# A graph network on one NeuronCore: a limit of two indirect DMAs in flight from GpSimd

## What is computed

```
L0:  radial = exp(coeff * (distance - offsets)^2)                  # 50 per edge
     h   = silu([x[src], x[dst], radial] @ Wm1 + bm1)
     h   = silu(h @ Wm2 + bm2);  message = h @ Wm3 + bm3
     out = segment_sum(message, dst)
     x   = layernorm(x + mlp([x, out]))                            # Wu1, Wu2, Wi1, Wi2
L1:  xt  = logmap0(x)
     att = sigmoid([xt[src], xt[dst], edge_attr_128] @ att_w + att_b)
     sup = xt + segment_sum(xt[src] * att, src)
              + mean by src of edge_attr_128 + mean by dst of edge_attr_128
     x   = layernorm(x + proj(expmap0(sup)))
```

## Time and profile before, and how to read it

| | |
|---|---|
| median of 3 runs | 2708.51 us (2707.11 to 2714.91) |
| profiled execution, span from first to last instruction | 2669.9 us |
| time outside the span, by difference to the median | 38.6 us |
| mean granted TensorE clock | 0.761 |
| busy: PE, DVE, POOL, ACT | 66%, 63%, 56%, 51% |
| DMA queue of POOL (software): packets, bytes, share of 16 engines | 50176, 104.07 MB, 13.2% |
| DMA queue of SP: packets, bytes, share | 283474, 233.47 MB, 33.7% |

### The profile page before, as it was taken

How to read it: one execution, slowest core, us unless ns; L and a number is a source line. 1 busy time by engine, 2 the same in 40 slices (tenths; PEclk the granted TensorE clock), 3 DMA queues, 4 the chain that set the end, 5 groups by cost and what they waited for, 6 DMA issues and landing times.

```text
span 2669.9 us, 41647 instructions
## 1 busy us (share of the span) xinstructions
PE 1766.1 (66%) x11127; PEld 1530.4 (57%) x11127; DVE 1679.0 (63%) x5490; ACT 1361.0 (51%) x3965; POOL 1498.9 (56%) x1572
## 2 busy tenths in 40 slices
PE   5677777777878787776643244777775666576770
PEld 5466665655666666565533233677665656576660
DVE  5666666666666677776535334788765555466668
ACT  3666665665666666875425333666643233233224
POOL 3566666665666666655566665566555455555510
PEclk8788888898888778997755556677777677777795
DMA  7465655654333233333433335566555455455541
GB/s 192 122 148 124 150 131 130 148 133 111 88 84 86 84 86 85 87 83 103 133 89 100 87 105 140 160 187 186 171 155 151 147 154 152 142 168 167 172 136 49
DMA packets 337140, 341.98 MB, mean 128 GB/s; under 512 B 67402, under 2 KB 266948, under 8 KB 336898
## 3 DMA queue, kind: packets, MB, share of 16 engines
q1 hardware_dynamic: 283474, 233.47, 33.7%
q0 software_dynamic: 50176, 104.07, 13.2%
q10 hardware_dynamic: 3248, 1.71, 0.3%
HBM read 246.14 MB, written 90.15 MB: 126 GB/s over the span
## 4 chain that ended last, share of the span: by engine, by line
PE 30%; DVE 20%; issue 17%; another core or an unknown queue 15%; ACT 11%; DVEq 3%; SPq 0%; DMA 0%; ACTq 0%
PE bank L1651 8%; PE bank L1010 5%; PE bank L1630 4%; PE bank L1311 3%; DVEq L758 3%; PE bank L1284 3%; PE bank L1324 3%; DVE rt L987 2%; ACT L1093 2%; ACT L779 2%; ACT ring L1093 1%; PE bank L1320 1%; DVE ring L1184 1%; DVE ring L978 1%
## 5 line engine op out<-in xcount | busy, mean ns | idle before, releaser
L933 POOL DMA_INDIRECT gtab<-ring,idx x784 | 753.9, 962 | 556.3 <-ACT ring L952 238.9
L1060 POOL DMA_INDIRECT ra<-ptab,gis x784 | 744.9, 950 | 491.6 <-issue 199.7
L1010 PE MATMUL bank<-ring 128*128 128x78 f32 x1568 | 299.9, 341 | 284.0 <-issue 220.9
L949 ACT ACTIVATE rt<-rt 128x254 f32<-128x254 f32 x536 | 215.4, 403 | 470.7 <-DVE rt L989 347.6
L1010 PEld LDWEIGHTS bank<-ring 128*128 128x128 f32 x1568 | 278.0, 258 | 306.6 <-issue 251.0
L1284 PEld LDWEIGHTS bank<-ring 128*128 128x128 f32 x1568 | 232.9, 215 | 175.9 <-issue 153.8
L1073 ACT ACTIVATE ring<-bank 128x512 f32<-128x512 f32 x196 | 116.3, 594 | 395.3 <-remote 349.0
L1284 PE MATMUL bank<-ring 128*128 128x78 f32 x1568 | 238.1, 293 | 103.4 <-issue 86.4
L1651 PE MATMUL bank<-ring 128*128 128x130 f32 x1312 | 230.7, 332 | 86.5 <-issue 67.2
L1630 PE MATMUL bank<-rt 128*128 128x126 f32 x1072 | 196.6, 328 | 108.0 <-issue 73.8
L1311 PEld LDWEIGHTS bank<-wm,ring 128*128 128x128 f32 x1568 | 250.7, 228 | 25.5 <-issue 10.9
(11 more groups left out here) (274 smaller groups left out, 3817.3 us busy)
## 6 DMA issues: line engine op xcount, KB each, us to landing
ring<-in_edge_attr SPq DMA_DIRECT2D x196, 256.0 KB
ring<-gtab SPq DMA_DIRECT2D x89, 393.0 KB
gtab<-ring SPq DMA_DIRECT2D x36, 687.8 KB
ra<-in_edge_weight SPq DMA_DIRECT2D x132, 128.0 KB
ring<-gtab SPq DMA_DIRECT2D x49, 327.5 KB
ring<-reld SPq DMA_DIRECT2D x196, 78.0 KB
ring<-gtab SPq DMA_DIRECT2D x49, 262.0 KB
ra<-ptab,gis POOLq DMA_INDIRECT x784
```

The costliest lines, as they stand in the source:

```text
L933: G.indirect_dma_start(out=gtab[group_of(i)][:, :], out_offset=bass.IndirectOffsetOnAxis(ap=idx[:, n, i:i + 1], axis=0), in_=row[i % NE][: ...
L949: k = S.activation(prl[i % NPR][:, n, :], prl[i % NPR][:, n, :], ACT.Identity, accum_out=lgs[i % 2][:, n:n + 1])
L1010: k = T.matmul(bk[:, 256:256 + W], row[i % NE][:, n, 0:H], od2[i % NO2][:, n, :], start=(first and n == 0), stop=(n == 3), skip_group_chec ...
L1060: G.indirect_dma_start(out=gp[i % NGP][:, n, :], out_offset=None, in_=ptab[:, :], in_offset=bass.IndirectOffsetOnAxis(ap=gis[:, n, i:i + 1 ...
```

## The change

FLY = 2 is new. Each indirect DMA of POOL now has a semaphore by its sub-tile n (0 to 3) in the place of one by its buffer, and ahead of each, POOL waits for the landing of the DMA two before it of the same kind. PE waits for each sub-tile just ahead of its transpose; SP's waits for scatters go by the four new semaphores.

```
+FLY = 2
...
-LAYER = (... tuple(f"gp{i}" for i in range(NGP))
+LAYER = (... tuple(f"gp{i}" for i in range(4))
...
-ROWS = (... tuple(f"sc{i}" for i in range(NE)) ...
+ROWS = (... tuple(f"sc{i}" for i in range(4)) ...
...
         def row_load(e, i):
             e0 = edge0(i)
             if i >= NE:
-                e.wait_ge(s[f"sc{i % NE}"], 64 * (i // NE))
+                slots_done(e, i - NE)
                 e.wait_ge(s["rp"], i - NE + 1)
...
         def slots_done(e, i):
-            for j in range(NE):
-                if i >= j:
-                    e.wait_ge(s[f"sc{j}"], 64 * ((i - j) // NE + 1))
+            for n in range(4):
+                e.wait_ge(s[f"sc{n}"], 16 * (i + 1))
...
+        def landed(e, name, k):
+            if k >= 0:
+                e.wait_ge(s[f"{name}{k % 4}"], 16 * (k // 4 + 1))
...
         def rows_pool(e, i):
...
             for n in range(4):
+                landed(e, "sc", 4 * i + n - FLY)
                 G.indirect_dma_start(
                     out=gtab[group_of(i)][:, :], out_offset=bass.IndirectOffsetOnAxis(ap=idx[:, n, i:i + 1], axis=0),
-                    in_=row[i % NE][:, n, :], in_offset=None).then_inc(s[f"sc{i % NE}"], 16)
+                    in_=row[i % NE][:, n, :], in_offset=None).then_inc(s[f"sc{n}"], 16)
...
         def layer_pool(e):
...
                     for n in range(4):
+                        landed(e, "gp", 4 * i + n - FLY)
                         G.indirect_dma_start(
                             out=gp[i % NGP][:, n, :], out_offset=None, in_=ptab[:, :],
-                            in_offset=bass.IndirectOffsetOnAxis(ap=gis[:, n, i:i + 1], axis=0)).then_inc(s[f"gp{i % NGP}"], 16)
+                            in_offset=bass.IndirectOffsetOnAxis(ap=gis[:, n, i:i + 1], axis=0)).then_inc(s[f"gp{n}"], 16)
...
         def layer_pe(e):
...
-                    e.wait_ge(s[f"gp{i % NGP}"], 64 * (i // NGP + 1))
                     for n in range(4):
+                        e.wait_ge(s[f"gp{n}"], 16 * (i + 1))
                         T.matmul(bk[:, n * P:(n + 1) * P], v[:, n, :], ident, start=(n == 0), stop=False, is_transpose=True,
                                  skip_group_check=True)
```

More of the change, by code:

```diff
@@ L174 @@
        "acc0", "lim") + tuple(f"pt{i}" for i in range(6))
-LAYER = (tuple(f"rb{i}" for i in range(3)) + tuple(f"qw{i}" for i in range(NQW)) + tuple(f"gp{i}" for i in range(NGP))
+LAYER = (tuple(f"rb{i}" for i in range(3)) + tuple(f"qw{i}" for i in range(NQW)) + tuple(f"gp{i}" for i in range(4))
          + tuple(f"wb{i}" for i in range(4))
@@ L180 @@
          "abt", "abc", "abw")
-ROWS = (tuple(f"ea{i}" for i in range(NE)) + tuple(f"sc{i}" for i in range(NE)) + tuple(f"wn{i}" for i in range(NWN))
+ROWS = (tuple(f"ea{i}" for i in range(NE)) + tuple(f"sc{i}" for i in range(4)) + tuple(f"wn{i}" for i in range(NWN))
         + ("odr", "bwp", "dm", "lb", "rp", "acce", "zacc"))
```

## The result

| | before | after |
|---|---|---|
| median | 2707.81 us (2692.44 to 2714.91, 4 runs) | 3064.18 us (3060.88 to 3067.35, 4 runs) |
| ratio | | 1.132, 95% interval 1.129 to 1.136 |
| span of the profiled execution | 2669.9 us | 3061.3 us (its own time 3063.1) |
| first gather, last gather, last scatter | 32.5, 1236.0, 2546.1 us | 32.0, 1481.9, 2955.1 us |

The kernel became 13% slower. The forecast was 2627 us, with a range up to 2880. By the starts in POOL's time line the gathers take 246 us more, the scatters (with the seam ahead of them) 163 us more, the end behind them 18 us less and the start 0.5 us less: together the 391 us between the spans. The medians are 356 us apart, since the profiled execution of before was quicker than any of the timed ones.

What follows compares the result with a forecast made beforehand. Taken as bound: indirect DMA issue at about 1.5 us, all sequencers late after some six in a row. +8 - 10 - 15 - 64 = -81 us gave a span of 2589, plus 38.6 outside it 2627 us; range 2370 to 2880.

Steps and rivals of the forecast that it cites:

- The bound before: All engines: after some six indirect DMAs in a row, sequencers see waits and instructions late until the DMAs have drained.
- Step (2): POOL's new wait: landing seen 2.24 us behind the start, so free at 2.50 us until the crawl begins.
- rival C: POOL's new wait always sees landings late, released when all in flight landed: pace 1.75 us, 2938 us; chance 0.27.
- part (5): SP's row loads L896 and unit loads L1414 wait on four semaphores: costs nothing, covered by SP's own idle time.
- Step (3): Shorter crawl where POOL paces, 1.51 us per DMA: gathers 0, scatters -10, -15 and -64 us.
- wrong altogether: Sign against the forecast: the crawl stays as long with two in flight, or DVE's pauses outlast POOL's.
- Step (1): POOL's wait ahead of 1566 of 1568 indirect DMAs: 0.01 us each when satisfied, 16 us in all, 8 per stage.
- Step (4): PE waits four times instead of once ahead of the transposes L1320, 588 more waits: at most 6 us, beside POOL's pace.
- Step (6): The prologue of 33 us and the 123 us behind the last scatter stay.
- 38.6 us "outside the span": Whole run: median 2708.51 lies 38.6 us above the profiled span, taken as time outside it and added to 2589.
- B: POOL in both stages: the crawl was the whole reason for 1.5 us, so pace 1.26 us, 2370 us; chance 0.20.
- D: Nothing moves: the wait is never late, or gathers give back what scatters win; 2709 us; chance 0.11.

Runs made afterwards that it cites:

- base: The kernel before, without any edit, run once more for a trace on a chip of 2120 us: 2122.0 us, ratio 1.0005.
- fly1: The changed kernel with FLY = 1, each indirect DMA waiting for the landing of the one just before: 5055.8 us, 2.384 times the kernel before.
- halfrows1: The changed kernel with FLY = 1 and each gather fetching only the first 64 of its 128 rows: 4991.5 us in a single execution.
- after2: The changed kernel, without any edit, on a chip where the kernel before takes 2121.1 us: 3063.9 us, ratio 1.442.
- fly4: The changed kernel with FLY = 4, so four in flight with the same waits and semaphores: 2280.9 us, 1.075 times the kernel before.
- chunk2: The kernel before with its own semaphores and one wait per chunk, chunk i for chunk i - 2, five to eight in flight: 2676.3 us, ratio 0.999.

## Why the prediction was wrong, step by step

**The bound before** was read half right. On the first chip POOL issues behind its own rate and all engines crawl behind some six DMAs in a row; base shows the same program without any of it. I took this for a law of the program, and so for something that the change could cure.

**Step (2) is the step that failed.** I took "as seen by a sequencer after four", 0.94 + 1.30 = 2.24 us, for the landing time, and so the wait for free at 2.50 us. That pause was the end of a wait for `h1p`, which PE raises; no landing was in it. fly1 shows the true size: a gather that flies alone lands a median of 2.56 us behind its start and the next starts 0.26 us later, 2.8 us in all, or 3.3 us over a chunk's seam. Even an undisturbed landing is late at 2.50 us. The trace before held no wait of POOL for a landing, so it bounded the price from below only (1.73 us, when the bytes move), and I placed it too near that end. Measured: in the changed kernel POOL is held in 62% of the gathers (225 of 362 and 242 of 392, counting gaps over 0.45 us), and there the release comes a median of 3.37 us (beside the fills) and 3.31 us (behind them) behind the start of the DMA waited for; in the scatters 3.74 us up to 1860 us and 3.85 us behind, never under 2.68. The break-even that rival C named, a landing seen over 3.2 us behind its start, was right, and the measured values lie beyond it.

The page of the Trainium skill that the prediction set beside this ("DMA: Bandwidth & Descriptors", section "Anatomy of one DMA — SWDGE (gpsimd) path") gives 2.0 us fixed plus the bytes, 2.15 us for 64 KB; fly1's gathers measure 2.56 us from start to landing. With halfrows1's 2.41 us that makes 0.15 us for 32 KB and some 2.26 us fixed. In kind the page is off here: it says that most of the fixed part is waiting for the write to be confirmed, but in fly1 the first byte of a gather moves a median of 1.65 us behind the start (1.54 for a scatter) and the landing comes 0.34 to 0.40 us behind the last byte. Most of the time lies ahead of the transfer.

**What I had not in the sum at all: the fills.** The row of L1041 was on the page (36 of 687.8 KB), and in the ticks of the gathers; part (5) looked at SP's queue and found it covered. The cover was POOL's lead of six chunks. With two in flight 39 waits of over 3 us in the gathers are paid in full: the gathers are 2.04 us apart beside the fills, 1.68 behind them. Of the 246 us that the gathers lost, (2.04 - 1.51) x 400, about 210, were lost in the stretch with the fills. The fills' own part is the distance to the quiet pace: (2.04 - 1.68) x 400, about 140 us by this estimate. The rest, and the scatters' 163 us, is the landing time of step (2). No run without the fills was made.

**Step (3), the crawl.** Most of it went: DVE's idle time "remote" ahead of the adds at line 1566 (1559 before) is 17.4 us for 156.4, ACT's ahead of line 1080 (1073 before) 89.0 us for 349.0. In after2, on a chip of 2120 us, no wait of any engine is marked remote, so what is left is the first chip's. The 17.4 are a single gap late in the scatters, where landings came quickly and POOL issued 11 DMAs in it; time lines of DVE and of POOL in the changed kernel, and behind the dots DVE's row at the same place in after2:

```profile
2939.76 0.42 DVE L1566 TENSOR_TENSOR ra<-ra,bank 128x260 f32<-128x260 f32 x1 [17.44 <-remote]
...
2940.43 0.43 DVE L1566 TENSOR_TENSOR ra<-ra,bank 128x260 f32<-128x260 f32 x1 [12.97 <-PE bank L1658]
```

```profile
2934.67 0.96 POOL L939 DMA_INDIRECT gtab<-ring,idx  x1 [0.33 <-issue]
2935.93 0.96 POOL L939 DMA_INDIRECT gtab<-ring,idx  x1 [0.30 <-issue]
2937.73 0.96 POOL L939 DMA_INDIRECT gtab<-ring,idx  x1 [0.83 <-issue]
2940.86 0.96 POOL L939 DMA_INDIRECT gtab<-ring,idx  x1 [2.17 <-issue]
```

The gap stands in after2 too, 12.97 us long, as work of PE and ACT between two banks; so only some 5 us of the 17.44 are a late release. Even so that, with the 89.0 us of ACT, is a piece of what the prediction said would be "wrong altogether": a crawl with two in flight. My reading of its going elsewhere is that POOL is held up too often to issue eight close together (the longest row without a pause over 0.45 us has six); no run separates that from the number in flight. Its end gave back nothing, since the engines that it freed then waited for POOL: PE for gathers (421.9 us at line 1327), ACT 632.7 us for DVE, whose own feed comes through POOL's pace.

**Step (1), a met wait**: 0.01 us was right or high (fly4). There are 1564 of them, not 1566: each kind leaves out its first two. What was put at nothing is a wait that isn't met, which adds 0.26 us behind the landing, and 0.74 to 0.78 ahead of a chunk's first DMA. **Step (4), PE's four waits**: PE's 421.9 us ahead of the transposes are POOL's lateness; in fly4's quiet gathers, with the same four waits, POOL keeps base's rate, so they cost nothing there. **Step (5)**: no cost of its own shows. **Step (6)**: 33 us stayed, the end is 106 us for 124. **The 38.6 us "outside the span"** were no such thing: the run's own time is 2 to 3 us over its span (3063.1 for 3061.3, base's 2122.5 for 2119.6). Most of the difference was that the profiled execution of before was quicker than the timed ones. The forecast doesn't suffer from it, since 2627 is the median less 81.

**The rivals.** C had the sign, the place, the row that shows it (idle time of POOL released by its own DMAs) and the threshold; its price, 2938, was 126 us short. Its reason (seen only when all in flight has landed) falls twice. fly1's single DMAs are seen behind 2.8 us and not 2.24. And in the changed kernel 285 of the 467 held gathers start under 3.5 us behind the one waited for, when the gather between them is at most 2.26 us old, younger than any gather of fly1 was at its landing (2.4). It had 0.27. B's pace of 1.26 us exists, on other chips, without the change. D fell.

**Left open**: what makes the crawl where it is, whether three or four in flight would end it there, and whether five or more cost anything on a chip without it. chunk2 shows that five to eight don't end it. Six runs were made for it and met chips without it.

## What to carry to other kernels

A limit of k indirect DMAs in flight turns the time to a landing into a pace: landing time over k, or POOL's own rate if that is slower. The division came out too low here. For two it gives 1.53 us in the quiet gathers and 1.52 in the scatters; measured were 1.68 and 1.88. Beside more traffic a landing takes longer: the third scatter of a chunk lands a median of 2.29 us behind its start in fly1 and 3.28 in after2, while the first gather of a chunk, in the quiet stretch, takes 2.55 and 2.56 us. So look for that time in a trace in which something waits for a landing, not in a pause that another engine ends, and add to it every large transfer that shares the DMA engines. Here it is about 3.1 us alone and 7 beside a fill, against an issue every 1.25 us: a limit of four costs 7.5% on a chip of 2120 us, and one of five to eight nothing on a chip of 2678 us, where POOL pauses anyway. Before building on a stall that nothing in the program explains, run the kernel on a second chip.

## What the runs showed that I had not expected

- The same program takes 2708 and 2678 us in two places and 2120 us on three other chips, with POOL's indirect DMAs 1.51 to 1.67 and 1.26 us apart; a version held back by landings takes 3064 us on either kind. The ratio of the change is 1.13 or 1.44 by where it ran.
- The landing time of an indirect DMA barely depends on its size: half of the rows and bytes save 0.15 of 2.56 us. Its first byte moves only 1.65 us behind the start, and POOL starts the next DMA 0.26 us behind a landing that it waited for.
- The granted TensorE clock follows the waits: a mean of 0.879 for base, 0.756 for after2 and 0.654 for fly1, and PE's busy time for the same 11127 matmuls goes from 1539 us (base) to 2266 us (fly1).
